# Expert weights of a decoder's routed layers fetched by gathers on GpSimd instead of by SP's loads

## What is computed

```
# layer 0: gates by three rounds of row and column normalisation, then the two largest
g = relu(einsum('btd,edf->btef', x, wg))
p = einsum('btd,edf->btef', x, wp)
all_out = einsum('btef,efd->bted', g * p, wo)
gathered = take_along_axis(all_out, topk_idx[..., None], axis=2)
return sum(gathered * topk_gates[..., None], axis=2)        # x is added once inside and once outside

# layer 2: the two largest of eight logits, softmax over the two
z = (x @ w1[e] + b1[e]) * (x @ w2[e] + b2[e])
s = silu(z @ wg[e] + bg[e])
out = out + we[..., None] * (s @ w3[e] + b3[e])
```

## Time and profile before

| | us |
|---|---|
| median of three runs (lowest, highest) | 1980.51 (1978.91, 1981.27) |
| the profiled execution | 1978.91 |
| its span | 1977.0 |
| TensorE busy in it | 1463.3 |
| VectorE, ScalarE, GpSimd busy | 1224.5, 934.8, 336.6 |
| the 92 gathers of x (line 1478) on GpSimd, busy | 87.1 |

### The profile page before, as it was taken

The page is one execution under the profiler, slowest core; times in us unless marked ns, Lnnn a source line. Parts: engine busy times, 40 slices in busy tenths (PEclk is TensorE's granted clock), DMA queues, the critical chain, the costliest instruction groups (busy, mean ns, idle before and its releaser), DMA issues. The chain is left out here.

```text
span 1977.0 us, 32359 instructions
## 1 busy us (share of the span) xinstructions
PE 1463.3 (74%) x11270; PEld 891.0 (45%) x11270; DVE 1224.5 (62%) x4051; ACT 934.8 (47%) x2009; POOL 336.6 (17%) x358
## 2 busy tenths in 40 slices
PE   5997978852854568995456599999974993677874
PEld 2554434431742443442234256666653881443432
DVE  7776468844344657776666477777763223657876
ACT  4554357643311335553622277777751440136655
POOL 3320011112533013320011000000002326002100
PEclk9999989975985779998557599999995995669995
DMA  3220013211651023220010000000003652003300
GB/s 118 50 50 2 0 22 49 33 33 47 168 117 28 1 48 49 49 39 19 0 55 0 11 6 6 6 12 7 1 8 99 205 174 56 1 16 45 53 2 21
DMA packets 60160, 84.53 MB, mean 43 GB/s; under 512 B 8353, under 2 KB 46497, under 8 KB 59489
## 3 DMA queue, kind: packets, MB, share of 16 engines
q1 hardware_dynamic: 55008, 72.24, 15.2%
q0 software_dynamic: 4992, 10.23, 2.6%
HBM read 51.18 MB, written 9.18 MB: 31 GB/s over the span
## 5 line engine op out<-in xcount | busy, mean ns | idle before, releaser
L638 DVE TENSOR_REDUCE maxs<-ps 128x4 f32<-128x1024 f32 x192 | 234.9, 1223 | 65.4 <-PE ps L966 64.0
L794 ACT ACTIVATE L_xattn_probs<-ps 128x1024 f32<-128x1024 f32 x192 | 196.5, 1023 | 85.5 <-PE ps L991 81.1
L3380 ACT ACTIVATE wide_pr<-wide_sc,wide_nm 128x256 f32<-128x256 f32 x256 | 127.0, 497 | 12.7 <-DVE wide_nm L3315 12.2
L1478 POOL DMA_INDIRECT moe_xs<-normed,moe_table x92 | 87.1, 947 | 173.7 <-DVE moe_table L1445 83.1
L966 PE MATMUL ps<-keys,L_xattn_qs 64*128 64x256 bf16 x768 | 75.5, 275 | 42.8 <-DVE maxs L638 37.5
L1007 PE MATMUL ps<-L_xattn_probs,values 128*32 128x256 f32 x1536 | 103.8, 388 | 0.0
L3287 DVE CUSTOM_DVE_ANT_0 wide_sc<-ps,wide_mask 128x256 f32<-128x256 f32 x256 | 93.8, 420 | 9.6 <-PE ps L3405 8.6
L3310 DVE COPY wide_prT<-ps 128x512 f32<-128x512 f32 x64 | 44.3, 692 | 82.5 <-PE ps L3418 82.3
L1884 DVE SCALAR_TENSOR_TENSOR moe_z_sb<-ps,moe_wt,moe_a_sb 128x256 f32<-128x256 f32 x46 | 22.3, 484 | 92.8 <-ACT moe_a_sb L1916 91.8
L991 PE MATMUL ps<-L_xattn_qm,keys 64*128 64x256 bf16 x768 | 74.7, 272 | 6.1 <-ACT L_xattn_probs L794 5.8
L3325 DVE TENSOR_SCALAR wide_pr<-wide_pr,wide_inv 128x256 f32<-128x256 f32 x256 | 75.6, 350 | 1.8
(11 more groups left out here) (640 smaller groups left out, 3744.6 us busy)
## 6 DMA issues: line engine op xcount, KB each, us to landing
moe_wt<-in_packed_experts SPq DMA_DIRECT2D x23, 707.0 KB
moe_wt<-in_packed_experts SPq DMA_DIRECT2D x23, 384.0 KB
keys<-L_xattn_k_parts SPq DMA_DIRECT2D x108, 64.0 KB
L_xattn_qs<-L_xattn_q_parts SPq DMA_DIRECT2D x108, 64.0 KB
expert_out<-moe_y SPq DMA_DIRECT2D x46, 128.0 KB
weights<-in_packed_L_xattn SPq DMA_DIRECT2D x2, 1316.0 KB, 7.6
keys<-L_attn_k_parts SPq DMA_DIRECT2D x36, 64.0 KB
L_attn_qs<-L_attn_q_parts SPq DMA_DIRECT2D x36, 64.0 KB
```

The source lines that it names most:

```text
L638: v.tensor_reduce(nm, ps[:, BANK_M:BANK_M + 2, :].rearrange("p j (t n) -> p j t n", t=2), AX.X, ALU.max, negate=True).then_inc(S("m_used"), 1)
L794: a.activation(probs[:, s % RING, :, :, :].rearrange("p j t n -> p j (t n)"), ps[:, BANK_P:BANK_P + 2, :], ACT.Exp, scale=HD ** -0.5)\
L1478: g.indirect_dma_start(self.xs[:, j % BUFS, h * P:(h + 1) * P], None, C.normed, bass.IndirectOffsetOnAxis(self.table[:, n:n + 1], 0))\
L3380: ins = a.activation(pr[:, s % 3, j, qt, :], sc[:, s % 2, j, qt, :], ACT.Exp, bias=nm[:, s % 2, n:n + 1], accum_out=sums[:, s % 2, n:n + 1])
```

## The change

`fetch` on GpSimd now issues the expert weights too, as one indirect gather of 128 rows for each slice: partition p of `wt` receives the row that `rows_of[p, j]` names. Its width is 768 floats (3072 bytes) in the first stage and 1414 floats (5656 bytes) in the second. The order on GpSimd is weights j, then the two x gathers of slice j. Weights 0 wait for `rows_ready` only; x 0 waits for the stored rows and for `table`. From slice 4 on, weights j wait for `y_ready` of slice j-4, and x j waits for `x_turned` as before. SP keeps only the stores of y. Buffers, semaphores of the transfers, arithmetic and the other engines' programs are as they were. The change holds for both expert stages.

```diff
--- before.py
+++ after.py
@@ -1468,9 +1468,15 @@
     def fetch(self, g):
 
         C, S = self.C, self.C.sem
-        g.wait_ge(S("normed_stored"), 16)
-        g.wait_ge(S("table_ready"), 1)
-        for j in range(SLICES):
+
+        def weights(j):
+            if j >= BUFS:
+                g.wait_ge(S("y_ready"), j - BUFS + 1)
+            g.indirect_dma_start(self.wt[:, j % BUFS, :], None, self.experts,
+                                 bass.IndirectOffsetOnAxis(self.rows_of[:, j:j + 1], 0))\
+             .then_inc(C.routed[f"w_loaded_{j % BUFS}"], 16)
+
+        def rows(j):
             if j >= BUFS:
                 g.wait_ge(S("x_turned"), j - BUFS + 1)
             for h in range(HALVES):
@@ -1479,24 +1485,24 @@
                                      bass.IndirectOffsetOnAxis(self.table[:, n:n + 1], 0))\
                  .then_inc(C.routed[f"x_loaded_{j % BUFS}"], 16)
 
-    def weights(self, sp, j):
-
-        row = sp.value_load(self.rows_of[0:1, j:j + 1], min_val=0, max_val=7 * P)
-        sp.dma_start(self.wt[:, j % BUFS, :], self.experts[bass.ds(row, P), :])\
-          .then_inc(self.C.routed[f"w_loaded_{j % BUFS}"], 16)
+        g.wait_ge(S("rows_ready"), 1)
+        weights(0)
+        g.wait_ge(S("normed_stored"), 16)
+        g.wait_ge(S("table_ready"), 1)
+        rows(0)
+        weights(1)
+        rows(1)
+        for j in range(2, SLICES):
+            weights(j)
+            rows(j)
 
     def keep(self, sp):
 
         C, S = self.C, self.C.sem
-        sp.wait_ge(S("rows_ready"), 1)
-        for j in range(BUFS):
-            self.weights(sp, j)
         for j in range(SLICES):
             sp.wait_ge(S("y_ready"), j + 1)
             sp.dma_start(C.expert_out[j * SLICE:(j + 1) * SLICE, :].rearrange("(h p) d -> p h d", p=P),
                          self.y[:, j % 2, :].rearrange("p (h d) -> p h d", d=D)).then_inc(C.routed[f"y_stored_{j % 2}"], 16)
-            if j + BUFS < SLICES:
-                self.weights(sp, j + BUFS)
 
     def turn_in(self, pe, j):
```

## The result

The changed kernel took **1996.17 us** (median of five runs, 1988.52 to 1997.55), the kernel before 1980.51 (five runs, 1978.91 to 1985.86): ratio **1.0059, 95% interval 1.0032 to 1.0087**. The forecast was 1980.9, the range ended at 1991. The prediction was wrong: slower, not the same.

What follows compares the result with a forecast made beforehand. TensorE was taken to set both expert stages' rhythms; +2.8 us in the first stage and -2.4 in the second's head gave +0.4 on the profiled 1978.91, so 1979.3, and 1980.9 as median (profiled run 1.6 below it); range 1977.5 to 1991.

Steps and rivals of the forecast that it cites:

- Price of a weight gather: On GpSimd, both stages: a wide gather costs the same as a narrow one, 0.94 us, 1.25 with its gap.
- Heads: Start of each expert stage, until slice 1's x is used: +0.3 us in the first, -2.4 in the second.
- Rhythm of the second stage: Second expert stage: GpSimd's 3.75 us fit into TensorE's period, which stays 4.80 us.
- Rhythm of the first stage: First expert stage: GpSimd sets the pace, then full DMA engines; +2.8 us, head included, bounds +0.1 and +5.7.
- steady pace of 3.75: First expert stage: GpSimd's three gathers take 3.75 us a slice against TensorE's 3.59, from 498 to 568.
- The sum: Whole kernel: +2.8 us for the first stage and -2.4 for the second's head make +0.4.
- Landing takes the slack: Slices of the first stage: x lands late behind its weights, period 4.16 us, +6 us, 1987; chance 0.06.
- GpSimd is held up by VectorE: First-stage slices: a VectorE copy of 0.42 us delays GpSimd on each of 19 slices, +8 us, 1989; chance 0.03.
- GpSimd without idle places: Expected sign in the first stage: GpSimd never idle from 498 to 568, a slice each 3.75 us.

Runs made afterwards that it cites:

- e11: The changed kernel once more, on a chip where the kernel before takes 1981 us; ratio 1.0070 to the kernel before.
- e12: The kernel before once more, unchanged, on a chip where it takes 1981 us; ratio 1.0011.
- e6: The changed kernel once more, on a chip where the kernel before takes 1946 us; ratio 0.9992 to the kernel before.
- e5: The kernel before once more, unchanged, on a chip where it takes 1946 us; ratio 1.0000.
- e2: Weight gathers in the second expert stage only, the first as in the kernel before; ratio 0.9992 to the kernel before.
- e9: Kernel before plus a third narrow gather of distinct rows per slice, no added wait, on a 1981 us chip; ratio 1.0165.
- e16: Kernel before plus a GpSimd memset of 128x1060 ahead of each slice's two row gathers, on a 1981 us chip; ratio 0.9991.
- e14: Changed kernel with each weight gather replaced by a register read and plain transfer on GpSimd, on a 1946 us chip; ratio 1.0046 to the kernel before.
- e3: Kernel before plus the changed kernel's wait for y and a third narrow gather repeating the first half's rows; ratio 1.0087.
- e15: Kernel before plus a third narrow gather of distinct rows per slice, no added wait, on a 1946 us chip; ratio 0.9990.

## Why the prediction was wrong

- **Price of a weight gather: right.** 0.94 us was taken, 0.95 measured; the rows at six and eleven times the width of x cost the same. This case's trace agrees with the page of the Trainium skill that was cited, DMA: Bandwidth & Descriptors ("Anatomy of one DMA — SWDGE (gpsimd) path").
- **Heads: right.** The first stage -0.2 where +0.3 was forecast, the second -2.1 where -2.4 was.
- **Rhythm of the second stage: right.** 4.80, and 104.8 us from first to last copy in every profile of the changed kernel.
- **Rhythm of the first stage: this step failed.** It was put at +2.8, with +5.7 as the bound; on the chip of the result it was **+16.2**, on the next late one +10.3 (e11 against e12). On a quiet chip the whole stage gave +2.6 (e6 against e5) and the kernel 0.9992 against a forecast of 1.0002. That the size fits there is in part luck: one profile each is a weak proof, as the unchanged stage was 97.4 in e2 and 99.1 in e5 (on late chips 96.8 to 102.5, the spread being in the empty slices at the end). Ahead of the empty slices e6's loss also came in two steps, where GpSimd's lead was used up (5.36 and 5.12 us between copies), and not as a steady pace of 3.75. The sum treated TensorE's work as something that GpSimd can delay only through data. It put at nothing, without a reason, that while gathers follow each other closely TensorE's counts rise late on such a chip, by 0.3 to 2.4 us in the changed kernel.
- **No rival had it.** "Landing takes the slack" had the right loop, over y j-4, but the wrong delay in it: the rows were there. "GpSimd is held up by VectorE" looked at the wrong pair of engines. "GpSimd without idle places" was wrong too: it waited at least 13.7 us for y in the first stage, and 7.4 in e6.
- **The profile of before had the sign.** Its return stretch has ACT idle 13.2 us with "remote" as releaser, until 9.3 us after the last matmul it needed, behind a GpSimd that gathers without a pause. The stages alone were read, since only they are edited. And in the first stage 1.1 us of each 3.59 were free of gathers, which is what the change fills. In the second stage the change leaves 1.05 of each 4.80 free, and no count was late there in either profile on a late chip.

Shown: that the loss comes with closely spaced gathers (e9 against e16), that it needs neither width nor the wait (e9), that a busy GpSimd alone doesn't make it (e16), and that it is absent on the three quiet chips. Not shown: what inside the chip holds the counts back, how far apart gathers must stand, whether it is the chip itself or its state at that time, and whether the recording of the semaphores has a part in it, as late counts and missing records come together.

## What to carry to other kernels

An engine's spare time may be what keeps another one fast: before filling GpSimd with gathers, look in the trace for places where it already gathers without a pause, and compare there the end of TensorE's last matmul with the start of the engine that waits for it. A releaser such as "remote" or a transfer of another layer is a sign to do that by hand. A count that seems late while its waiter starts on time is more likely a missing record. A difference of half a per cent from one chip is a statement on that chip; run both kernels on another before explaining it.

## What the runs showed of the hardware

- With gathers in a row on GpSimd, TensorE's matmuls were answered up to 2.4 us late in the slices of the changed kernel, 9.0 us in the head of e9 and 9.3 us in the return stretch of before. Such answers stand in the profiles of all three late measurements and in none of the three quiet ones.
- A gather of 128 rows costs GpSimd 0.94 to 0.95 us at 512, 3072 and 5656 B.
- A slice with a register read and a plain transfer in the gather's place takes GpSimd 3.58 us (493.23 to 496.81 in e14), against 3.75 with three gathers: the pair adds 1.08 us to the two x gathers' 2.50, a gather 1.25.
- More gathers of one repeated row went with full DMA engines: a share of 0.95 at 135 GB/s in e3, against 0.65 at 137 GB/s in e15, which lacks the wait for y as well.
